# Where POOL issues the third norms' scales, and where ACT and DVE issue their last squares, statistics and probabilities, in a fused adaLN attention and mixture-of-experts layer

## The reference

```python
h = layernorm(x) * (1 + ca) + sa
# linear attention, 8 heads of 16
q = h @ Wq;  K = Q = elu(q) + 1;  V = q / L
msg = (Q @ sum(K^T V)) * Z * L;  msg = msg @ Wm        # Z = 1 / (Q . sum(K))
y = h + layernorm(msg, g1, b1)
y = y + layernorm(relu(msg @ W1) @ W2, g2, b2)
x = x + ga * y                                          # "x1" below
h = layernorm(x) * (1 + cb) + sb                        # the third norm
# 8 experts, each takes its 512 tokens of highest probability
probs = softmax(h @ Wg)
...                                                     # top 512 tokens of each expert
out = out + gate_e * (gelu(h @ W1[e]) @ W2[e])          # over the experts
x = x + gb * out
```

## Time and profile before

| | |
|---|---|
| median of three executions | 232.7 us |
| the profiled execution | 233.51 us |
| its span, first to last instruction | 231.7 us |
| PE busy | 175.6 us, 76% |
| DVE busy | 171.6 us, 74% |
| POOL busy | 152.0 us, 66% |
| ACT busy | 132.4 us, 57% |
| granted TensorE clock, mean | 0.895 of full speed |

### The profile page before, as it was taken

The page is one execution under the profiler, slowest core; times in us unless marked ns, Lnnn a source line. Parts: engine busy times, 40 slices in busy tenths (PEclk is TensorE's granted clock), DMA queues, the critical chain, the costliest instruction groups (busy, mean ns, idle before and its releaser), DMA issues.

```text
span 231.7 us, 4342 instructions
## 1 busy us (share of the span) xinstructions
PE 175.6 (76%) x1161; PEld 138.6 (60%) x1161; DVE 171.6 (74%) x661; ACT 132.4 (57%) x425; POOL 152.0 (66%) x236
## 2 busy tenths in 40 slices
PE   0779898999999998965664869877589989985000
PEld 0536676888778887854333446555379879974000
DVE  1889988699998798998988989998018997554000
ACT  2149985367647897854987853332547667851000
POOL 8698837357266868454799950057777787777771
PEclk9999999999999999975577577999999999999555
DMA  5995000000100000000176222013343352111110
GB/s 166 263 280 200 3 0 1 0 3 0 46 3 0 4 0 0 1 3 0 39 203 204 83 82 74 0 33 104 91 112 91 98 127 81 46 61 45 57 45 23
DMA packets 16967, 15.49 MB, mean 67 GB/s; under 512 B 1904, under 2 KB 14320, under 8 KB 16944
## 3 DMA queue, kind: packets, MB, share of 16 engines
q1 hardware_dynamic: 14288, 9.70, 14.0%
q0 software_dynamic: 2240, 5.51, 8.1%
q10 hardware_dynamic: 416, 0.01, 0.1%
HBM read 8.92 MB, written 6.29 MB: 66 GB/s over the span
## 4 chain that ended last, share of the span: by engine, by line
PE 34%; DVE 33%; POOL 15%; issue 7%; ACT 6%; DMA 2%; POOLq 1%; DVEq 0%; ACTq 0%
POOL out_dram L422 7%; PE pH L974 6%; DVE scr L1315 6%; PE pQ L983 6%; DVE x_sb L1190 4%; POOL yr L287 4%; DVE bn L1022 3%; PE pQ L881 3%; DVE rows L1030 2%; POOL rs L287 2%; DMA x_sb<-in_L_attn_x_dram 2%; PE pH L871 2%; DVE mv L1025 2%; PE pH L804 1%; DVE featT L1044 1%
## 5 line engine op out<-in xcount | busy, mean ns | idle before, releaser
L419 POOL DMA_INDIRECT rows<-table_dram,gidx x28 | 30.0, 1072 | 24.2 <-DVE gidx L1407 16.0
L422 POOL DMA_INDIRECT out_dram<-rows,gidx x28 | 27.3, 976 | 8.5 <-issue 6.7
L974 PE MATMUL pH<-x_sb,hid 128*128 (+1 forms) x140 | 22.5, 283 | 1.1 <-ACT hid L637 0.9
L983 PE MATMUL pQ<-ew,u 128*128 (+1 forms) x140 | 22.2, 281 | 1.2 <-ACT u L651 0.8
L373 POOL TENSOR_TENSOR scr<-feat,z 128x512 f32<-128x512 f32 x8 | 8.8, 1098 | 18.0 <-DVE z L1167 18.0
L983 PEld LDWEIGHTS pQ<-ew,u 128*128 128x128 f32 x140 | 18.4, 191 | 3.0 <-issue 1.9
L651 ACT ACTIVATE u<-pH 128x256 f32<-128x256 f32 x35 | 13.4, 384 | 11.5 <-PE pH L974 11.4
L1456 DVE SCALAR_TENSOR_TENSOR t<-pQ,wslot,scr 128x128 f32<-128x128 f32 x35 | 12.2, 347 | 10.5 <-PE pQ L983 10.0
L974 PEld LDWEIGHTS pH<-x_sb,hid 128*128 128x128 f32 x140 | 18.4, 191 | 2.3 <-issue 2.1
L524 ACT ACTIVATE sqj<-pQ 128x128 bf16<-128x128 f32 x60 | 15.8, 281 | 6.6 <-PE pQ L815 3.0
L287 POOL TENSOR_TENSOR yr<-yv,neghalf 128x4 f32<-128x4 f32 x16 | 17.6, 1099 | 1.3
(11 more groups left out here) (331 smaller groups left out, 530.8 us busy)
## 6 DMA issues: line engine op xcount, KB each, us to landing
table_dram<-x_sb SPq DMA_DIRECT2D x9, 256.0 KB, 2.8
x_sb<-in_L_attn_x_dram SPq DMA_DIRECT2D x8, 256.0 KB, 5.6
table_dram<-rows SPq DMA_DIRECT2D x7, 256.0 KB, 2.4
ew<-in_L_ffn_W_dram SPq DMA_DIRECT2D x2, 512.0 KB, 9.1
w1d<-in_L_ffn_W_dram SPq DMA_DIRECT2D x1, 1024.0 KB, 10.4
rows<-table_dram,gidx POOLq DMA_INDIRECT x28, 2.8
out_dram<-rows,gidx POOLq DMA_INDIRECT x28, 2.2
wmod_sb<-in_L_wmod_dram SPq DMA_DIRECT2D x1, 384.0 KB, 4.7
```

The costliest lines, as they stand in the source:

```text
L419: gp.indirect_dma_start(row[:, t, :], None, table[:, :], bass.IndirectOffsetOnAxis(gidx[:, t:t + 1], 0)).then_inc(gathered[t], 16)
L422: gp.indirect_dma_start(out.rearrange("b l d -> (b l) d"), bass.IndirectOffsetOnAxis(gidx[:, t:t + 1], 0), row[:, t, D:2 * D], None).then_ ...
L974: mm = te.matmul(pH[i % 2][:, f * P:(f + 1) * P], wcur[:, i % RW, f * P:(f + 1) * P], xt[:, bass.ds(i - e, 1), :], start=True, stop=True)
L983: mm = te.matmul(pQ[i % 2][:, 0:D], eh[:, i % 2, f * P:(f + 1) * P], ew[:, bass.ds(e, 1), f * D:(f + 1) * D], start=(f == 0), stop=(f == 1))
```

## The change

Three loops are written in another order, one each on POOL, ACT and DVE. No instruction is added, removed or altered.

```diff
@@ POOL, second phase
             for s in range(G + 5):
                 if s < G:
                     qprime(s)
-                if 0 <= s - 5 < G:
-                    rs3(s - 5)
                 if 0 <= s - 2 < G:
                     yrs(s - 2, 0, "sq1", "yr1_done")
                 if 0 <= s - 3 < G:
                     yrs(s - 3, 1, "sq2", "yr2_done")
+                if 0 <= s - 5 < G:
+                    rs3(s - 5)
@@ ACT, second phase
                 if s == G + 1:
                     a_soft(0)
-                if s == G + 2:
+                if G < s <= G + 2:
                     a_square(s - 3, 1, "y2_ready", "sq2")
                 if 0 <= s - 6 < ACT_ROWS:
                     a_xn3(s - 6)
-                if 0 <= s - 3 < G - 1:
+                if 0 <= s - 3 < G - 2:
                     a_square(s - 3, 1, "y2_ready", "sq2")
@@ DVE, second phase
-                if 0 <= s - 4 < G - 2:
+                if 0 <= s - 4 < G - 1:
                     v_stats3(s - 4)
...
-                if s == G + 1:
-                    v_probs(0)
                 if 0 <= s - 3 < G:
                     v_u2(s - 3)
...
-            v_stats3(G - 2)
             v_stats3(G - 1)
+            v_probs(0)
             v_kept(0)
```

## The result

The changed kernel takes 240.4 us (median of 4 runs, 239.2 to 240.6) against 232.8 us (4 runs, 232.7 to 233.8). The ratio is 1.030, with a 95% interval of 1.028 to 1.033: slower by 7.0 us (6.5 to 7.6), or 7.6 us between the medians. The forecast was 238.7 us, slower by 6.0, with a range to 241.5. The sign, the mechanism and the places came as forecast. The size is 1.0 us too small by the ratio, 1.6 by the medians. The profiled execution took 240.34 us with a span of 238.6 and a mean granted clock of 0.887; before it was 233.51, 231.7 and 0.895.

What follows compares the result with a forecast made beforehand. The prediction took a ring of waits between DVE and POOL, about 7 us a turn, to bound the kernel. Terms 3.6 + 1.4 + 1.0 + 0.0 = 6.0 us on 232.7 gave 238.7 us, range 235.9 to 241.5.

Steps and rivals of the forecast that it cites:

- The ring: Loop between DVE and POOL: rs last puts nm and x1's first half into each turn, steps 6 to 8; 3.6 us.
- strict reading: SBUF port rule taken literally: one POOL stage slowed in each turn beside DVE's residual instructions, some 0.5 us more per turn.
- The logits of batch 0: DVE step 8: they wait for rs(3), now behind a branch scale that needs ACT's squares; 1.4 us, bounds none to 1.9.
- nm(4) behind rs(4): DVE step 9: nm(4) waits for rs(4), behind group 6's branch 2 matmuls and squares; 1.0 us, bounds 0 to 1.6.
- ACT's new order: ACT in step 9: squares ahead of the normed rows, counted as saving 1.64 us against the old order.
- DVE's moves: Probabilities go behind x1(7), statistics of group 6 ahead of it: zero for the logits, x1(7) 0.3 us later but covered.
- The delay reaches the end: Behind 108.11 us every engine waits for the keys and the change touches nothing, so the whole 6.0 us stays.
- The sum: Terms of 3.6, 1.4, 1.0 and 0.0 us added to 6.0 us, for a median of 238.7 us.
- PE covers it: Rival: PE is full in the stretch and hides DVE's lateness; nothing changes, 232.7 us; chance 0.04.
- Faster: Rival: branch scales come early and nm does not hold DVE; its waits go, 230.5 us; chance 0.05.
- only the ring: Rival: squares come early enough, waits of steps 8 and 9 vanish, only the 3.6 us remain, 236.3 us; chance 0.12.
- The clock: Rival: PE idles at the end of step 8, its clock falls early and matmuls slow; 3.9 us more, 242.6; chance 0.11.

## Why the prediction was right, and where its size was off

- *The ring, 3.6 us.* Right: 3.8 in the profile after. The seven rs of the trace from 73.38 to 109.67 us took 1.01 us each, but this says little about the SBUF rule, since in steps 6 to 8 DVE stands idle, waiting for this very rs. What met DVE's residual instructions now were small yv: those at 71.32 and 87.81 took 0.61 us instead of 0.19 and ended 0.06 us after DVE's L1136, which ran from 71.18 and 87.67 for 0.69 us. The rule of the Trainium skill ("SBUF — State Buffer", section "SBUF: two separate sides"), by which the later of the two stands still, fits these two. It does not fit DVE's L1132, which started at 78.92 beside a yr that ran from 78.79 to 79.80 and took its usual 0.68. The 0.5 us more per turn of its strict reading did not come.
- *The logits of batch 0, 1.4 us.* Right: a wait of 1.53, and 1.6 in the table.
- *nm(4) behind rs(4), 1.0 us.* This is the term that was too small. From the logits to the last logits the changed kernel loses 1.3 + 0.7 = 2.0 us, and 1.2 in the kernel with one filling matmul, where the clock held. The forecast had ACT's squares done at 100.8 and nm(4) at 103.7. In that kernel the squares end at 102.0 and nm(4) starts at 104.76, or 104.45 without its start offset of 0.31. So 0.8 us are missing even at 2.4 GHz: 0.4 had come with the ring and the logits, and the rest I lost by taking 1.8 us from u to the end of the branch 2 matmuls, where 2.02 and the ways between the engines stand. In the changed kernel itself the clock adds 0.8, which makes 105.25.
- *ACT's new order, counted as 1.64 us saved in that term.* Wrong, but it did no harm to the sum. With the old order, in the kernel with POOL's edit alone, ACT wrote the rows from 99.16 to 100.8, while PE's branch 2 matmuls ran to 100.6. The squares ended at 101.8. In the new order, in the kernel with one filling matmul, ACT waits 1.43 us for PE and ends them at 102.0. Counted from x1(1) both end after 35.6 us. The rows had stood in idle time. I should have asked what ACT would do in the gap. The prediction also named ACT's gaps "none of weight", and in step 9 of the changed kernel they are 2.28 and 1.85 us, in waits for PE.
- *DVE's moves, 0.0.* Right in the totals (240.09 without them, 240.38 and 240.37 with them). In the traces they cost: from nm(4) to the last logits the changed kernel takes 10.3 us and the one with POOL's edit alone 9.4, since the probabilities no longer fill the wait for rs(4). The forecast had this in its nm(4) term.
- *The delay reaches the end.* Right within the scatter of the traces. From the first search instruction to the end of the span the fourteen traces took 119.3 to 120.5 us, that of the kernel before 120.2.
- *The sum.* 6.0 forecast, 7.4 at the last logits in the trace: 0.6 from the terms and 0.8 from the clock, with little of it visible in the total, 7.0. Counted from x1(1), the last logits are 7.4 and 7.3 us late in the two traces of the changed kernel, 6.6 with one filling matmul and 5.9 with POOL's edit alone, and the 1.2 us by which the rest of the kernel differs from trace to trace can hide such differences. That the clock makes part of the surplus is shown for the traces. How much of it is in the medians stays open, because the kernels that differ in it (240.07, 240.38, 240.37, 240.09) can't be told apart.
- *The range.* It held, but its upper end was not what the text calls it: the forecast with half the clock's 3.9 us is 240.7, not 241.5.
- *The rivals.* "PE covers it" is refuted. PE was full from 69 to 76 us before and is full there after as well (7.00 of 7.00), and a delay on DVE and POOL, both less busy, still reached the end. Its gaps open later: from 84 to 88 us PE is busy for 2.80 us, where it was 4.00. The prediction had this rival win by the Trainium skill ("Perfetto Trace Analysis", section "Identifying the Most-Contended Engine"), and read it too narrowly. The page works on the engine of highest occupancy first, but judges TensorE by its flops and weight loads and not by its matmul time. By weight loads PE is at 6.04 of 7.00 us in the earlier trace rows, and DVE, at 6.40, is the busier. Neither reading gives the loss, which is made of waits. "Faster" fell with nm's waits, "only the ring" with the logits' wait. "The clock" came in part.

## What to carry to other kernels

Moving an instruction to the end of a producer's step cost nothing by itself here (233.31 us with both consumers moved, ratio 0.999). Its price is set by where its consumers stand in their in-order queue and by what is queued behind them, so follow every consumer of the moved result, not only the nearest; here there were two, nm and the logits. A ring over two engines that are not the busiest can set the time. On it, a consumer of the producer's last result at the head of the next step was the costly place, 3.8 us in three turns, and one place earlier on the producer's side was free.

## What the hardware showed unexpectedly

The same gaps on PE do not always bring the clock down. Two stretches of the changed kernel, 92 to 96 and 96 to 100 us (the columns are those of the earlier trace rows):

```profile
92.00:96.00 4.00, 2.04 (x16) 1.64 (x15) 3.09 (x14) 2.48 (x11) 2.01 (x5) 0.99 0.00 0
96.00:100.00 4.00, 4.00 (x12) 2.21 (x11) 3.15 (x11) 1.24 (x9) 1.83 (x3) 0.59 0.00 2
```

The same stretches with POOL's edit alone:

```profile
92.00:96.00 4.00, 2.04 (x17) 1.64 (x16) 2.89 (x13) 2.25 (x11) 2.01 (x5) 1.00 0.00 0
96.00:100.00 4.00, 3.37 (x20) 2.09 (x19) 3.38 (x12) 3.16 (x14) 1.75 (x3) 1.00 0.01 2
```

And with nm behind z:

```profile
92.00:96.00 4.00, 0.95 (x4) 0.27 (x3) 2.24 (x7) 1.75 (x7) 2.60 (x5) 1.00 0.00 0
96.00:100.00 4.00, 4.00 (x38) 4.00 (x38) 3.93 (x18) 2.18 (x12) 0.87 (x2) 1.00 0.01 2
```

PE was busy for 2.04 us of the first stretch in two kernels, and the clock fell in one of them (0.59) and stayed at 2.4 GHz in the other. With the logits alone moved it was 2.04 us again, and the clock held. In the third kernel shown PE was busy for only 0.95 us, and the clock held too. The times of that kernel lie far apart, 234.9 us at a mean clock of 0.892 and 237.4 and 237.3 at 0.878 and 0.879. That the clock spreads them is not shown: with rs last in steps 5 to 7 a run at 0.887 took 236.8 us and one at 0.895 took 239.1.

Two smaller things. A filling matmul of 512 columns in fp32 stands in the trace as two instructions, 1.02 us together at 2.4 GHz. And POOL's small scaling instruction, 0.19 us as a rule, took 0.61 at 71.32 and at 87.81 us beside DVE's L1136.
